# Spectral mixing: operands turned on chip, one matmul per mode column for eight mode rows, and modes stored for reads of 1 KB

## The reference

```python
X = dht2d(x)                      # real part minus imaginary part of fft2
Xr = flip_periodic(X)
Xc, Xrc = X[:, :, sl_h, sl_w], Xr[:, :, sl_h, sl_w]          # 64 x 64 modes
kernel, kernel_rev = weight, flip_periodic(weight)           # weight: [32, 32, 64, 64]
x_even, x_odd = (Xc + Xrc) * 0.5, (Xc - Xrc) * 0.5
total = einsum('bixy,ioxy->boxy', x_even, kernel) + einsum('bixy,ioxy->boxy', x_odd, kernel_rev)
out = dht2d(pad(total), is_inverse=True) + bias
```

## Time and profile before

| | us |
|---|---|
| Median of 3 runs (4851.97 to 4865.74) | 4859.74 |
| The profiled execution's own time | 4849.25 |
| Its span | 4847.5 |
| Stage of the convolutions, 0 to 3292 | 3292 |
| Forward transform, 3292 to 3825 | 533 |
| Mixing, 3825 to 4157 | 332 |
| Inverse, from 4157 | 690.5 |

### The profile page before, as it was taken

The page is one execution under the profiler, slowest core; times in us unless marked ns, Lnnn a source line. Parts: engine busy times, 40 slices in busy tenths (PEclk is TensorE's granted clock), DMA queues, the critical chain, the costliest instruction groups (busy, mean ns, idle before and its releaser), DMA issues. The chain is left out here.

```text
span 4847.5 us, 126300 instructions
## 1 busy us (share of the span) xinstructions
PE 4411.3 (91%) x43186; PEld 2810.0 (58%) x43186; DVE 3693.8 (76%) x5717; ACT 2549.6 (53%) x4890; POOL 1718.5 (35%) x1963
## 2 busy tenths in 40 slices
PE   4999999999999999999999999995777667899999
PEld 2555555555555554555555545554666567788887
DVE  5777877778777787787877777777888798665555
ACT  2666656566666565666666556664777300233333
POOL 4455454554545545455454554543000000000000
PEclk9999999999999999999999999997999887899999
DMA  5867667676676766766767667678888899799999
GB/s 141 198 150 181 167 150 190 147 184 167 151 183 168 169 169 149 180 169 165 181 152 186 156 157 186 151 186 257 312 302 312 206 183 185 278 408 408 411 411 393
DMA packets 730988, 1042.28 MB, mean 215 GB/s; under 512 B 149184, under 2 KB 612832, under 8 KB 680928
## 3 DMA queue, kind: packets, MB, share of 16 engines
q1 hardware_dynamic: 658064, 1011.11, 74.9%
q10 hardware_dynamic: 72784, 29.63, 2.5%
HBM read 746.67 MB, written 293.88 MB: 215 GB/s over the span
## 5 line engine op out<-in xcount | busy, mean ns | idle before, releaser
L350 PE MATMUL bank<-ring_B,w_now 128*64 128x512 f16 (+1 forms) x14283 | 3100.7, 378 | 86.9 <-DVE ring_B L292 61.2
L350 PE MATMUL bank<-ring_A,w_now 128*64 128x512 f16 (+1 forms) x14283 | 3100.7, 378 | 0.0
L350 PEld LDWEIGHTS bank<-ring_B,w_now 128*64 128x64 f16 x14283 | 1551.9, 110 | 1530.1 <-issue 81.6
L350 PEld LDWEIGHTS bank<-ring_A,w_now 128*64 128x64 f16 x14283 | 1551.8, 110 | 3.5
L288 ACT COPY ring_B<-ring_A 64x516 f32<-64x516 f32 x1059 | 657.8, 621 | 943.0 <-DVE ring_A L574 912.1
L574 DVE SCALAR_TENSOR_TENSOR ring_A<-bank,ring_A 128x512 f16<-128x512 f32 (+1 forms) x1027 | 700.6, 682 | 468.0 <-ACT ring_A L418 448.6
L418 ACT ACTIVATE ring_A<-bank 128x512 f16<-128x512 f32 (+1 forms) x1027 | 601.9, 586 | 278.7 <-PE bank L350 276.9
L728 POOL TENSOR_TENSOR ring_A<-xn,ring_A 128x512 f16<-128x512 f32 x515 | 586.1, 1138 | 94.6 <-POOL xn L726 93.0
L1421 DVE SCALAR_TENSOR_TENSOR i_ot<-i_ob,i_bias_bc,i_xt 128x512 f32<-128x512 f32 x512 | 365.7, 748 | 281.5 <-DMA i_xt<-x 170.2
L1365 PE MATMUL i_ob<-i_back,i_u 128*128 128x256 f32 x2048 | 528.0, 380 | 5.0 <-DVE i_ot L1421 5.0
L290 ACT COPY ring_B<-ring_A 64x516 f32<-64x516 f32 x705 | 438.4, 622 | 8.1
(11 more groups left out here) (161 smaller groups left out, 5068.9 us busy)
## 6 DMA issues: line engine op xcount, KB each, us to landing
f_xt<-x SPq DMA_DIRECT2D x128, 1024.0 KB, 6.8
i_xt<-x SPq DMA_DIRECT2D x128, 1024.0 KB, 16.0
out<-i_ot SPq DMA_DIRECT2D x128, 1024.0 KB, 14.2
st_in_A<-in_x SPq DMA_DIRECT2D x65, 1024.0 KB, 7.3
st_in_B<-in_x SPq DMA_DIRECT2D x65, 1024.0 KB, 7.8
x_in_A<-in_x SPq DMA_DIRECT2D x324, 192.0 KB, 3.9
res_A<-in_x SPq DMA_DIRECT2D x324, 192.0 KB, 5.2
res_B<-in_x SPq DMA_DIRECT2D x324, 192.0 KB, 5.0
```

Source lines behind the costliest of these rows:

```text
L350: last = nc.tensor.matmul(dst[64 * half:64 * half + 64, 0:nb * IMG], w_now[n][:, w, 64 * dx:64 * dx + 64], r[side][:, kind, s0:s0 + nb, dx ...
```

## The change

The order of modes in DRAM becomes [half, part, sample, channel, row, column], so that four rows of one channel are 1 KB in one piece; ACT's store is split by part, in pieces of 256 B. The weights of chunk 0 and of chunk 1 are loaded in the forward stage, four rows each for the four partition blocks (real lower, real upper, imaginary lower, imaginary upper), and POOL no longer turns them. In the mixing stage, ACT (real part) and DVE (imaginary part, mirrored) copy the loaded weights into `wt[p, column, row and out]`, POOL copies the modes into `ft[p, column, row, half, sample]` and multiplies by a 0 or 1 of the half, and PE makes one matmul of 128x128 weights and 128 columns per mode column; of its 128x128 result the four 32x32 blocks with equal row are taken, one by DVE and three by ACT. The work goes in quarters of 16 columns; `wt` and `ft` are refilled a quarter at a time, while raw loads have two buffers. Two tables of constants change their row order, and the result's rows lie as [sample, half, row]. The inverse is otherwise as before.

```diff
+def load_weights(engine, w, k, raw, here):
+    lo, n = M - ROWS * (k + 1) + 1, ROWS if k else ROWS - 1
+    dst = lambda p, r, m: raw[p * C:(p + 1) * C].rearrange("p (o t) x -> p o (t x)", t=ROWS)[:, :, r * M:(r + m) * M]
+    src = lambda y, m: w[:, :, y:y + m, :].rearrange("i o t x -> i o (t x)")
+    engine.dma_start(dst(0, 0, ROWS), src(ROWS * k, ROWS)).then_inc(here, 16)
+    engine.dma_start(dst(1, 0, n), src(lo, n)).then_inc(here, 16)
+    engine.dma_start(dst(2, 0, n), src(lo, n)).then_inc(here, 16)
+    engine.dma_start(dst(3, ROWS - n, n), src(ROWS * k + ROWS - n, n)).then_inc(here, 16)
+    if not k:
...
@@ build_forward
-            turn_rows(copy, wt, wr)
...
                 for m in range(2):
-                    act.dma_start(fv[s, :, m, 4 * half:4 * half + 4, :], fs[half][:, m]).then_inc(f_out[half], 16)
+                    for part in range(2):
+                        act.dma_start(fv[m, part, s, :, 4 * half:4 * half + 4, :], fs[half][:, m, :, part * M:(part + 1) * M]
+                                      ).then_inc(f_out[half], 16)
...
-            load_weights(act, w, 0, wt, w_here)
-            load_opposite(act, w, 0, wr, w_here)
+            for k in range(2):
+                load_weights(act, w, k, w_raw[k], w_here)
@@ build_mix
+            for k in range(NCK):
+                if k >= 2:
+                    sp.wait_ge(ft_ready, (k - 1) * NQ)
+                for part in range(2):
+                    for g in range(2):
...
+                        sp.dma_start(to_rows(own, T - own), rows(T * k + own, T - own)).then_inc(f_here[buf], 16)
+                if k >= 2:
+                    sp.wait_ge(re_ready, (k - 1) * NQ)
+                    sp.wait_ge(im_ready, (k - 1) * NQ)
+                    load_weights(sp, w, k, raw[buf], w_here[buf])
...
+            for n in steps:
+                pe.wait_ge(re_ready, n + 1)
+                pe.wait_ge(im_ready, n + 1)
+                pe.wait_ge(ft_ready, n + 1)
+                if n >= 2:
+                    pe.wait_ge(taken_dve, n - 1)
+                    pe.wait_ge(taken_act, n - 1)
+                for x in range(XQ):
+                    kx = n % NQ * XQ + x
+                    last = nc.tensor.matmul(bank[n % 2][:, x, :], wt[:, kx, :], ft[:, kx].rearrange("p t g b -> p (t g b)"),
+                                            start=True, stop=True)
+                last.then_inc(made, 1)
...
+            for n in steps:
+                take(dve, nc.vector.tensor_copy, (0,), n, taken_dve)
+                if n + NQ in steps:
+                    imaginary(n + NQ)
...
+            for n in steps:
+                take(act, nc.scalar.copy, (1, 2, 3), n, taken_act)
+                if n + NQ in steps:
+                    real(n + NQ)
+                if n >= NQ and n % NQ == 0:
+                    store(n // NQ - 1)
+            store(NCK - 1)
...
+            for n in steps:
+                if n + NQ in steps:
+                    pool.wait_ge(made, n + 1)
+                    modes(n + NQ)
```

More of the change, by code:

```diff
@@ L787, in spectral_constants @@
     by_pair = np.concatenate([np.arange(0, IMG, 2), np.arange(1, IMG, 2)])
-    back_h = np.concatenate([c.T, s.T], 0)[:, by_pair]
+    i = np.arange(M // 2)
+    below = i - i % ROWS + ROWS - 1 - i % ROWS
+    ky = np.concatenate([i, np.where(below, M - below, M // 2)])
+    back_h = np.concatenate([c.T[ky], s.T[ky]], 0)[:, by_pair]
     back_w = np.concatenate([(c + s).T, (c - s).T], 0) / (IMG * IMG)
@@ L927, in _ @@
             for half in range(2):
-                sp.wait_ge(f_out[half], 32 * S + 1)
+                sp.wait_ge(f_out[half], 64 * S + 1)
             sp.wait_ge(mid_out, 16 * S + 1)
+            sp.wait_ge(w_here, sum(W_DMAS))
         @block.tensor
@@ L1112, in take_f @@
                 if k == 0:
-                    act.wait_ge(f_out[half], s * 32 + 1)
+                    act.wait_ge(f_out[half], s * 64 + 1)
                 act.wait_ge(f_ps[buf], n + 2)
@@ new lines, in quarter, with weights_here, take @@
+        def quarter(n):
+            return slice(n % NQ * XQ, (n % NQ + 1) * XQ)
+        def weights_here(engine, n):
+            k = n // NQ
+            if k >= 2 and n % NQ == 0:
+                engine.wait_ge(w_here[k % 2], W_DMAS[1] * (k // 2))
+        def take(engine, copy, rows, n, taken):
+            k = n // NQ
+            engine.wait_ge(made, n + 1)
+            if k >= 2 and n % NQ == 0:
+                engine.wait_ge(gone[k % 2], 32 * (k // 2))
+            for t in rows:
+                p = slice(t * C, (t + 1) * C)
+                last = copy(to[k % 2][p, :, quarter(n)], bank[n % 2][p, :, t * 2 * S:(t + 1) * 2 * S].rearrange("p x c -> p c x"))
+            last.then_inc(taken, 1)
@@ new lines, in store @@
+            def store(k):
+                act.wait_ge(taken_dve, (k + 1) * NQ)
+                act.wait_ge(taken_act, (k + 1) * NQ)
+                for g in range(2):
+                    act.dma_start(t_d[:, g, T * k:T * k + T].rearrange("b t o x -> (t o) b x"), to[k % 2][:, g * S:(g + 1) * S, :]
+                                  ).then_inc(gone[k % 2], 16)
+            for n in range(NQ):
+                real(n)
+            for n in steps:
[4 more added lines that the diff above has]
+                    store(n // NQ - 1)
@@ new lines, in _, with modes @@
+            store(NCK - 1)
+        @block.gpsimd
+        def _(pool):
+            for i in range(4):
+                for g in range(2):
+                    last = nc.gpsimd.memset(half_is[i * C:(i + 1) * C, g:g + 1], 1.0 if i % 2 == g else 0.0)
+            last.then_inc(masks, 1)
+            pool.wait_ge(masks, 1)
+            def modes(n):
+                k = n // NQ
+                if n % NQ == 0:
+                    pool.wait_ge(f_here[k % 2], 16 * (4 * (k // 2 + 1) + (2 if k % 2 == 0 else 0)))
+                src = f_raw[k % 2][:].rearrange("p b t x -> p x t b")[:, quarter(n)]
+                for g in range(2):
+                    last = nc.gpsimd.tensor_scalar(ft[:, quarter(n), :, g, :], src[:, :, ::-1, :] if g else src, half_is[:, g:g + 1], None, ALU.mult)
+                last.then_inc(ft_ready, 1)
+            for n in range(NQ):
+                modes(n)
+            for n in steps:
+                if n + NQ in steps:
+                    pool.wait_ge(made, n + 1)
+                    modes(n + NQ)
```

172 lines of the change are left out of this document (59 added, 113 removed).

## The result

The changed kernel takes 4908.05 us (median of 5 runs, 4894.40 to 4916.02), the kernel before 4859.74 us (5 runs, 4847.57 to 4865.74). The ratio is 1.0098, with a 95% interval of 1.0079 to 1.0116: slower by some 48 us, more than the 0.3% that can be told from no change, and above the range of 4795 to 4872. The sign was forecast wrong.

What follows compares the result with a forecast made beforehand. The prediction took nearly full DMA queues (share 1.02) to bound the mixing stage. Mixing -65, forward start +11 and mode stores +30 summed to -24 us against the profiled 4849.25, set against the median 4859.74 as 4836 us; range 4795 to 4872.

Steps and rivals of the forecast that it cites:

- the term for the stores of the modes, +30 us: Forward stage: two more stores per half sample cost ACT 0.94 us, unhidden, 32 times; +30 us (15 to 34).
- rival 3: Forward stage: ACT's queue lacks room for four stores, ACT stands still at each; +106 us, total 4912 us; chance 12%.
- Its sign, issues over 1 us each: Forward stage: store issues over 1 us each on ACT would show that its queue was short of room.
- The forward stage's start, +11 us: More weight loads ahead of ACT's first conversion, 20.5 us, less some 10 us from POOL no longer turning rows; +11 us.
- The mixing stage, -65 us: Mixing stage ends at 4091 in place of 4157, with DMA setting its pace; -65 us (-106 to -30).
- POOL's 8 x 1.6 us a chunk: Mixing stage: POOL's eight masked copies of 1024 take at most 1.6 us each, 13 us a chunk, under the DMA's time.
- the one gap of 4 us: Mixing stage: loads of chunk 2's modes wait 4 us until POOL has read chunk 0's; the only gap expected.
- The DMA's 34 us a chunk: Mixing stage: weights 19.5, modes 9.8 and stores 4.8 us make 34 us of DMA a chunk, which sets the pace.
- That strided copies cost nothing: Mixing stage: copies reading elements 1 KB apart were charged nothing for the step, judged from small 32-element copies.
- rival 4: Mixing stage: strided copies cost double or more, so it gains only 30 to 37 us; total 4867 us; chance 12%.
- Rival 1: Mixing stage: bound by PE and DVE after all, it falls to ACT's 17 us a chunk; total 4737 us; chance 4%.
- The stores' smaller pieces at the DMA: Forward stage: mode stores falling from 512 to 256 B pieces were expected to add nothing at the DMA.

Runs made afterwards that it cites:

- stores_512x4: Changed kernel, modes stored by four DMAs of 512-byte pieces a half sample, still from ACT: 4861.35 us against 4848.18 for the kernel before (1.0026).
- w1_sync: Changed kernel, chunk 1's weight loads moved from the start of ACT's queue to SP among the image loads: 4894.11 us against 4848.18 for the kernel before.
- modes_dve: Changed kernel, masked copies of the modes moved from POOL to DVE: 4846.00 us against 4848.18 for the kernel before (0.9996).
- before_w01: Kernel before, mixing chunks 2 to 7 reusing the weights of chunks 0 and 1 instead of loading theirs: one run of 4853.27 us, mixing stage 329.5 us.
- stores_sync: Changed kernel, its four mode stores a half sample issued by SP instead of ACT: 4763.35 us against 4851.42 for the kernel before (0.9818).
- before_stores_sync: Kernel before, its two mode stores a half sample issued by SP instead of ACT: 4792.30 us against 4852.43 for the kernel before (0.9871).

## Why the prediction was wrong

**The step that failed is the term for the stores of the modes, +30 us.** It took 32 pairs of two more stores at the 0.94 us of the earlier trace rows and put the queue's shortage of room down as rival 3, at 12%. Measured, it is +79 us: the first sample's two groups took 4.93 and 3.53 us in place of 0.99 and 0.94 (6.5 us more), and the 15 steps from sample to sample grew from 456.5 to 529.3 us. Of that, 37 us are the two more DMAs, close to the forecast (stores_512x4), and 42 us the smaller pieces, twice as many. With this miss alone (49 us) the kernel would have taken some 4885 us, outside the range; with the mixing stage's alone (28 us), some 4864, inside it. The argument against rival 3, that these stores are 128 KB and the slow weight loads 1 MB, looked at bytes. The runs vary pieces with bytes fixed: a half sample has 1024 pieces before and 2048 after, and a weight load of 1 MB in runs of 1 KB has 1024 too. Whether the issue waits for room in a queue or for the pieces to be worked out was not separated by a run. Two things speak for the first: the standing becomes worse beside SP's loads (w1_sync), and at the stage's start a load of 1 MB in 1024 pieces is issued in 1.07 us when loads of 256 KB stand ahead of it (3331.27), and another in 4.95 us behind loads of 1 MB (3336.45).

**Rival 3 had the mechanism, and its time partly by luck.** It put the mixing stage at -65 us and the stores at +106; measured are -37 and +79, two misses of 28 and 27 us that cancel. Its sign, issues over 1 us each, did not appear: four issues in 3.3 us are 0.8 us each, against 0.47 before.

**The forward stage's start, +11 us, was right as a sum.** The middle row of the first sample came 16.7 us later; less the 6.5 us of its stores that is 10. Both parts were forecast too large: the loads delay the first conversion by 17.2 us and not 20.5, which leaves 7 us and not 10 for what POOL's absence gives back.

**The mixing stage, -65 us, was wrong in two terms that partly cancel; measured -37.**
- POOL's 8 x 1.6 us a chunk was 8 x 4.2. It made the one gap of 4 us into some 27: two chunks of modes, 4.2 MB, are loaded by about 3938, and the DMA moves nothing from 3940 to 3963. It also kept POOL going to 14 us before the end of the stage. The price was doubled from a copy of another form; 1.65 of the 3.68 us are the form and 0.84 the step. The other 0.5 us of the mean of 4.21 came beside DVE's copies of weights.
- The DMA's 34 us a chunk was 29.5 where nothing else held it back. With the DMA's pace in modes_dve and without POOL's the stage takes 242 us, 24 less than forecast.

**That strided copies cost nothing was wrong for long ones.** Rows of 32 elements could not show it. On POOL the step costs 0.84 us per 1024. ACT's copies of 2048 took 3.72 us against the 2.5 called an upper bound; no run took ACT's step away. DVE's of 1920 elements took 3.41 us, above the 3 us that were to be their limit. Of rival 4 this much is right, with POOL as the one engine where it reached the path. The rule of the Trainium skill that was weighed there (SBUF — State Buffer, Specifications (TRN2)) had the better sign.

**What bound the stage before was misread.** The DMA share of 1.02 was taken for a full DMA. before_w01 shows PE and DVE taking turns at 36.9 us a chunk, and the first reading, in the earlier trace rows, had been the right one. Rival 1's premise held, though not its time, since the DMA comes next at 29.5 us.

**The stores' smaller pieces at the DMA** were rightly costed at nothing: with SP issuing, a sample takes 27.0 us with pieces of 256 bytes (stores_sync) and with 512 (before_stores_sync). The Trainium skill (DMA: Bandwidth & Descriptors, Specifications) asks for 512; no loss shows here, where DVE sets the pace. It is the issuer that pays.

## What to carry to other kernels

Put stores on a queue whose engine nobody waits for: that alone was worth 52 us before the change and 133 after. Count what a DMA issue costs by DMAs and by pieces, not by bytes alone, and by what stands in the queue ahead of it. Price an instruction only from a row of the same form, operations and access pattern included. A DMA share of 1 does not say that the DMA is the bound; leave bytes out and see whether the stage moves.

## What was not expected of the hardware

- On POOL, a tensor_scalar with one operation takes 2.84 us for 1024 float32 elements, with two operations 1.20 us.
- In the changed kernel's trace POOL's copies take 4.80 us on the mean beside DVE's copies of weights, and 3.72 us without them.
- The recorded DMA share goes to 1.14, at 248 GB/s, for loads that alone move 215 and 184 GB/s.
- While PE reads float32 operands with a step of 1 KB, DVE's evictions go from 0.67 us to 6 us (median in the trace before; longest 7.83). In the changed kernel PE reads neighbours, and DVE's evictions (of 32 partitions in place of 128) take 0.68 us beside its work. Whether it is the reading or PE's 512 short matmuls was not tried apart.
